# A gather's wait, moved from a sum to the products behind it, in an edge pass on one core

## The reference, cut to what matters

```
def _gnn_layer(edge_index, x, edge_attr, norm, We, be, Wn, bn):
    src, dst = (edge_index[0], edge_index[1])
    parts = [x[src], x[dst]]
    if edge_attr is not None:
        parts.append(edge_attr)
    e = relu(concatenate(parts, axis=-1) @ We + be)
    msg = e * norm[:, None]
    agg = segment_sum(msg, dst, num_segments=x.shape[0])
    x_new = relu(concatenate([x, agg], axis=-1) @ Wn + bn)
    return (x_new, e)
```

## Time and profile before

| | us |
|---|---|
| median of 3 runs | 2657.64 |
| profiled execution | 2663.59 |
| its span, first to last instruction | 2661.8 |
| granted TensorE clock, mean over the span | 0.859 |
| POOL busy | 1090.6 (41%) |
| PE busy | 2071.4 (78%) |
| DVE busy | 1371.3 (52%) |

### The profile page before, as it was taken

The page is one execution under the profiler, slowest core; times in us unless marked ns, Lnnn a source line. Parts: engine busy times, 40 slices in busy tenths (PEclk is TensorE's granted clock), DMA queues, the critical chain, the costliest instruction groups (busy, mean ns, idle before and its releaser), DMA issues. The chain is left out here.

```text
span 2661.8 us, 44629 instructions
## 1 busy us (share of the span) xinstructions
PE 2071.4 (78%) x13051; PEld 1491.6 (56%) x13051; DVE 1371.3 (52%) x4392; ACT 627.3 (24%) x1221; POOL 1090.6 (41%) x1087
## 2 busy tenths in 40 slices
PE   7677779999999657777777668888878677777775
PEld 5322234444544346666656567777776566666663
DVE  6989932232332445555555445555555354445455
ACT  0147831121221122222222312222223111111111
POOL 0566500000000036656655346666663555555551
PEclk7678889999999777777777889999999777888887
DMA  1024540000000343333333245555553333333331
GB/s 62 15 58 91 105 39 0 0 0 0 0 0 0 116 149 105 100 98 106 104 99 100 89 132 160 162 160 162 163 159 107 99 100 93 98 97 99 93 94 48
DMA packets 173243, 230.29 MB, mean 87 GB/s; under 512 B 47275, under 2 KB 103238, under 8 KB 172406
## 3 DMA queue, kind: packets, MB, share of 16 engines
q1 hardware_dynamic: 138470, 157.99, 20.1%
q0 software_dynamic: 34144, 63.45, 9.9%
q10 hardware_dynamic: 432, 6.29, 0.6%
HBM read 144.77 MB, written 63.22 MB: 78 GB/s over the span
## 5 line engine op out<-in xcount | busy, mean ns | idle before, releaser
L1609 POOL DMA_INDIRECT rows<-p_dram,src_i x960 | 916.2, 954 | 680.6 <-PE psum L1720 298.6
L1838 DVE TENSOR_TENSOR agg_t<-psum,agg_t 128x128 f32 x1260 | 359.7, 286 | 420.3 <-remote 291.6
L1696 PE MATMUL psum<-q_parts,hot_all 128*128 x2880 | 353.3, 233 | 161.7 <-issue 143.1
L1700 PE MATMUL psum<-w_c,before 128*128 128x128 f32 x1680 | 415.7, 328 | 48.7 <-issue 47.7
L1771 ACT ACTIVATE rows<-rows 128x512 f32<-128x512 f32 x240 | 151.3, 631 | 980.8 <-DVE rows L1831 705.3
L1720 PE MATMUL psum<-hot_w,rows 128*128 128x128 f32 x1920 | 330.1, 313 | 66.4 <-issue 61.9
L1696 PEld LDWEIGHTS psum<-q_parts,hot_all 128*128 128x128 bf16 x2880 | 255.2, 104 | 211.3 <-issue 186.1
L1720 PEld LDWEIGHTS psum<-hot_w,rows 128*128 128x128 f32 x1920 | 292.4, 225 | 98.0 <-issue 95.7
L982 PE MATMUL psum<-adj,parts 128*128 (+2 forms) x1750 | 339.7, 351 | 5.1 <-ACT agg L1061 4.4
L1822 DVE TENSOR_SCALAR hot_w<-col_f,dst_loc,weight 128x128 f32<-128x128 f32 x960 | 341.2, 359 | 0.9
L1831 DVE TENSOR_TENSOR rows<-psum,rows 128x512 f32<-128x512 f32 x240 | 164.6, 686 | 309.3 <-remote 273.2
(11 more groups left out here) (293 smaller groups left out, 2262.9 us busy)
## 6 DMA issues: line engine op xcount, KB each, us to landing
e_dram<-after SPq DMA_DIRECT2D x210, 256.0 KB
before<-e_dram SPq DMA_DIRECT2D x210, 256.0 KB
adj<-stage SPq DMA_DIRECT2D x196, 97.8 KB
rows<-p_dram,src_i POOLq DMA_INDIRECT x960
pair_rows<-sorted_rows SPq DMA_DIRECT2D x75, 128.0 KB
hot_all<-dst_rows SPq DMA_DIRECT2D x1, 4096.0 KB, 13.1
hot_all<-dst_rows ACTq DMA_DIRECT2D x1, 3072.0 KB, 18.4
p_dram<-p_sb SPq DMA_DIRECT2D x6, 384.0 KB
```

What stands on the lines that cost most here:

```text
L1609: nc.gpsimd.indirect_dma_start(out=rows[:, b % ROWS, m * D:(m + 1) * D], out_offset=None, in_=p_dram, in_offset=bass.IndirectOffsetOnAxis( ...
L1696: mm = nc.tensor.matmul(o, hot, t["q_parts"][:, bass.ds(window, 1), part, :], start=(part == 0 and i is None), stop=(part == 2 and e_befor ...
L1700: mm = nc.tensor.matmul(o, before[:, q % BEFORE, m * P:(m + 1) * P], w_c[:], start=False, stop=True)
L1838: nc.vector.tensor_tensor(a, psum[:, A_BANKS[q % len(A_BANKS)], m * P:(m + 1) * P], a, ALU.add).then_inc(agg_on, 1)
```

## The change

```
             for b in range(REST_QUADS):
                 if b == 1:
                     further_rows()
-                if b >= ROWS:
+                if b >= ROWS and slot_of(b) - 1 == slot_of(b - 1):
+                    pool.wait_ge(spread, slot_of(b - ROWS) + 4)
+                elif b >= ROWS:
                     pool.wait_ge(summed, slot_of(b - ROWS) + 1)
                 elif b >= 2:
                     pool.wait_ge(spread, slot_of(b - 2))
```

## The result

| | before | after |
|---|---|---|
| median of 3 runs, us | 2657.64 | 2789.66 (2787.27 to 2794.79) |
| profiled execution, us | 2663.59 | 2794.79 |
| its span, us | 2661.8 | 2793.0 |
| granted clock, mean over the span | 0.859 | 0.834 |

A forecast was written before the change was run, and what follows sets the result against it. No engine is full: a loop of waits bounds the passes, with PE nearly standing during POOL's gather runs. Pass 2 +41 us and passes 1 and 3 +10 make +51, 2709 us; range 2640 to 2780.

The forecast's parts named there:

- nothing: All passes: gathers have slack, so a start up to 2.9 us later is hidden; time stays at 2658 us; chance 0.16.
- The second quad (slot 28) now waits for products(26): Pass 2, second quad: starts at 1661.94, after these products are issued, 0.98 us later than before.
- The third quad was given 0.5: Pass 2, third quad: its products are already issued, so the delay is 0 or 2.2 us; 0.5 taken.
- the run of eight behind the sorted slot: Pass 2, quad after a sorted slot: POOL may save 0.96 us, but two quads join; group 21.5 us against 18.60, +2.9.
- PE's loss of 5.7 us: All passes: PE nearly stands late in a run of eight gathers, losing 5.7 us against 0.85 in a run of four.
- 0.11 us a matmul: PE's pace, from 41 matmuls in 4.5 us, used to price its work and its losses during runs of gathers.
- The later start itself is hidden: Passes 1 and 3, second quads: start 2.88 and 2.66 us later, but rows are needed only at the add, after the release.
- +0.2: Passes 1 and 3: cost taken per group in us, 48 groups, +10 us together.
- The upper end: Passes 1 and 3: all three quads form one run of twelve, release 1.7 us later, +1.7 us a group.
- Runs everywhere: Rival: quads join into twelve in passes 1 and 3, eight in pass 2; +152 us, 2809 us; chance 0.12.
- Torn runs: Rival: in passes 1 and 3 each quad becomes a run by itself, pass 2 unchanged; -63 us, 2595 us; chance 0.14.

The follow-up runs named there:

- e13: The kernel before with an unused tile and semaphore, in the set where the kernel before took 2318.41 us: 2316.73 us, ratio 0.9996.
- e15: The change in passes 1 and 3 alone, in the set where the kernel before took 2318.41 us: 2317.97 us, ratio 1.0001.
- e1: The kernel before with the new wait before second quads of a group only: 2735.72 us, ratio 1.0287.
- e2: The kernel before with the new wait before third and fourth quads of a group only: 2647.72 us, ratio 0.9955.
- e10: The kernel before with a POOL pause of about 2 us before second quads' gathers, plus unintended waits before other quads: 2772.59 us, ratio 1.0351.
- e11: The kernel before with that pause before third and fourth quads, passes 1 and 3, plus unintended waits in all passes: 2721.47 us, ratio 1.015.

## Why the prediction was wrong

The direction and the place were right: slower, by POOL's waits, most of it in pass 2, and the reading that POOL's gathers hold TensorE was borne out: the rival "nothing", which needs TensorE undisturbed, is just what the set of e13 to e15 shows. The size was not. By pass:

| | forecast | its ends | measured |
|---|---|---|---|
| pass 1 | +5 | −14 to +41 | +6 |
| pass 2 | +41 | +12 to +70 | +80 |
| pass 3 | +5 | −49 to +41 | +41 |

The range of the whole, 2640 to 2780, took 40 us as the upper end of passes 1 and 3 together, where the terms give 41 for each. By the terms' own ends the sum reaches 2810, and the measured 2789.66 lies inside; the range was too narrow for its own terms.

**The step that failed, pass 2.** "The second quad (slot 28) now waits for products(26). These are issued until 1661.23 + 0.44 = 1661.67": the later event was priced from a trace in which each quad is a run by itself, so that PE had those products half issued when it was released; 0.98 us. The third quad was given 0.5, and the run of eight behind the sorted slot was priced apart, by PE's loss of 5.7 us. But the run of eight, once there, changes what the first price is made of: PE comes out of it one slot further behind, and the products asked for are not begun (1719.2 to 1725.3 above). Over pass 2 the mean idle time before the first gather of a second quad went from 2.0 to 6.4 us, +4.4 and not +1.0, while before third quads it stayed (1.38 and 1.28) and before first quads fell (1.74 and 0.91). 4.4 − 0.1 − 0.8 = 3.5 us a group, times 24 is 83; the forecast had 1.7. The two terms were added where the run makes the wait longer. e1 and e2 show it apart: each brings the runs of eight by itself (25 and 20 of them in pass 2), and POOL's mean idle time before second quads goes from 2.0 to 4.1 us in e1 and to 3.9 in e2, though there second quads still wait for the old sum. They cost 41 and 39 us, so in this pass the prices of the two waits do add up; what didn't was the forecast's own split into a wait and a run.

**A term that was left out: the clock.** The forecast took PE at 0.11 us a matmul in all cases. In pass 2 the granted clock fell from 0.94 to 0.82, in the stretch shown to 0.60, and where a matmul of this form takes 275 ns in the median at the full clock (2.4 GHz; before, 1660.9 to 1665.4, granted 1.00) it takes 421 at the lower level (1.2 GHz). Leave out of pass 2 all stretches of over 0.6 us from one matmul's start to the next: what is left grew by 31 us, 393 to 425, with no work added, and the stretches left out grew by 48. The share depends on where the limit is put (13 us with 0.3 us, 39 with 1.0), so as an estimate the clock had between a sixth and a half of the pass's loss. Whether the fall is wholly a result of the standing was not tested by itself: the six kernels with pass 2 at 513 to 528 us have it at 0.90 to 0.94, the nine above 550 us at 0.82 to 0.88, which is a match and not a proof.

**Pass 3.** "The later start itself is hidden" failed, and with it "+0.2". The upper end was +1.7 a group, one run of twelve with the release 1.7 us later, and it is what was measured: 41 / 24 = 1.7. That is luck: the mechanism is not quite that one. Twelve runs of twelve do appear, and DVE's first instruction comes 3.3 us after their last gather, where it came 2.7 us after that of a run of eight in before (medians). But most of the loss is that the second quad then waits for the sorted slot's products: 10.8 us from the last gather to the next, 2343.13 to 2353.96, where the earlier trace rows have 5.9. Over pass 3 the mean idle time before second quads went from 4.0 to 7.0 us. e1 puts the second quad's wait alone at +35. e10, with the old event and 2 us more before second quads, cost +3 in pass 3, so a delay of that size does not account for it there; for passes 1 and 2 e10 and e11 are not clean enough to say what a bare delay costs.

**Pass 1** came out as forecast, +6, and that is luck too: each wait alone made it shorter (−10 and −25), which no term of the forecast has, and +6 is no more than separates two executions of a pass with the same waits (550 and 543 us above).

**Rivals.** "Runs everywhere" named 2809 us and 70 us for pass 2: near in size, and the runs of twelve are there in pass 3 (twelve of them), but in pass 1 there is one more than before, and its price per run was not the one that counts. "Torn runs" gives the third quad's wait a gain in passes 1 and 3, and e2 has such a gain, 25 and 32 us, when the second quad's wait stays old. But the runs were not torn (24 of eight in pass 3, with it and without), so what came true is the size, for one half of the change, and not the mechanism.

The Trainium skill (SBUF — State Buffer, "Who interferes with whom") says that PE never waits on anyone and that a DMA does not contend with a compute engine. The forecast set it aside for the earlier trace rows. The set of e13 to e15 agrees with it, with 66 matmuls in 6.9 us of gathers; the traces of before and after do not, with 11 to 13. Which of the two holds is a matter of the set and not of the kernel.

## What to carry to other kernels

When two engines take turns, ask of a later wait not how much later the event is in today's trace, but what the waiting engine's partner will have left undone when the new wait is met; prices taken from a state that the change itself ends can be far too low, as here 1.0 us against 4.4. A change with one form in several stages is several changes: here the same line costs 80 us in one pass, its one half gives 32 in another, and choosing by pass, with one buffer more, gave a kernel 2.2% faster than the one before. When a test inserts a branch, read the whole chain of conditions again: two of the tests here changed waits that they were meant to leave alone. Run the kernel before again beside each set, since its own time moved from 2658 to 2318 us for a reason outside the program.

## What the runs showed of the hardware

- POOL's indirect gathers (954 ns each, 0.30 us between two) can hold TensorE nearly still: 11 to 13 matmuls in 6.8 to 6.9 us late in a run of eight. With plain DMAs of as many bytes from POOL, of consecutive rows (549 ns each), the whole kernel takes 2081.5 us and not 2678.6.
- The same gathers at the same 952 ns did not hold it in one set of runs out of six, and the kernel before took 2318.4 us there, some 340 us less, nearly all of it in the three passes. What makes the difference is not known.
- One more row buffer gave nothing (1.0012, 0.9995 to 1.003), though POOL stands idle for 680.6 us between its gathers, most of it until a buffer is free.
